# Slot attention inside one large kernel: the per-group tail work is put in other places on PE, ACT, DVE

## The reference, cut to what matters

```python
q  = slot_query                              # 16 slots, D = 256, the same for 32 batches
o  = q + mha(q, x, x, d_Wq, ..., d_Wo, d_bo)  # 16 heads; x: 32 batches of 64 tokens
h  = layernorm(o, e_ln_g, e_ln_b)             # per slot
u  = silu(h @ e_W1 + e_b1);  g = silu(h @ e_Wg + e_bg)     # 16 experts, one per slot
o  = o + (u * g) @ e_W2 + e_b2
out = mha(x, o, o, c_Wq, ..., c_Wo, c_bo)
```

## Time and profile before

| | us |
|---|---|
| median of 3 runs | 900.05 |
| lowest, highest | 898.2, 902.98 |
| the profiled execution | 898.2 |
| its span, first to last instruction | 896.2 |
| PE busy, of the span | 806.1 (90%) |
| DVE, ACT, POOL busy | 580.4, 511.6, 200.6 |
| first scores of `slots` / last work of `slots` / first expert matmul | 695.1 / 756.3 / 757.8 |

### The profile page before, as it was taken

The page is one execution under the profiler, slowest core; times in us unless marked ns, Lnnn a source line. Parts: engine busy times, 40 slices in busy tenths (PEclk is TensorE's granted clock), DMA queues, the critical chain, the costliest instruction groups (busy, mean ns, idle before and its releaser), DMA issues. The chain is left out here.

```text
span 896.2 us, 20582 instructions
## 1 busy us (share of the span) xinstructions
PE 806.1 (90%) x8104; PEld 696.4 (78%) x8104; DVE 580.4 (65%) x966; ACT 511.6 (57%) x954; POOL 200.6 (22%) x256
## 2 busy tenths in 40 slices
PE   5488999999999878999999998999997997997797
PEld 5278999999999756777778887999997995463454
DVE  3666777877877548888678884455443786331496
ACT  4138797888888526667577784433332454442354
POOL 0031433443433222244221223000000020000052
PEclk8689999999999989999999999999999999999899
DMA  7048676866876122442131103000000956999532
GB/s 301 6 167 307 249 257 225 308 229 219 288 271 212 49 76 55 87 89 47 37 135 33 49 25 103 39 2 1 1 1 12 409 242 222 423 426 420 204 93 72
DMA packets 70567, 143.20 MB, mean 160 GB/s; under 512 B 42521, under 2 KB 48153, under 8 KB 62921
## 3 DMA queue, kind: packets, MB, share of 16 engines
q1 hardware_dynamic: 64368, 127.25, 39.9%
q0 software_dynamic: 4496, 12.53, 4.0%
q10 hardware_dynamic: 1608, 2.12, 0.7%
HBM read 128.38 MB, written 13.50 MB: 158 GB/s over the span
## 5 line engine op out<-in xcount | busy, mean ns | idle before, releaser
L541 POOL DMA_INDIRECT results_of_experts<-k_w_ff,moew_place_of x39 | 53.5, 1371 | 148.8 <-DVE k_w_ff L769 86.9
L87 PE MATMUL moe_pH<-moe_hh,moew_wh 128*128 128x256 f32 x256 | 72.5, 283 | 2.4 <-DVE moe_hl L760 2.4
L89 PE MATMUL moe_pH<-moe_hl,moew_wh 128*128 128x256 f32 x256 | 71.7, 280 | 0.0
L88 PE MATMUL moe_pH<-moe_hh,moew_wl 128*128 128x256 f32 x256 | 71.7, 280 | 0.0
L760 DVE TENSOR_TENSOR moe_hl<-k_w_ff,moe_hh 128x512 fp32r<-128x512 f32 x64 | 44.3, 692 | 29.8 <-ACT moe_hh L697 29.8
L688 ACT ACTIVATE k_w_ff<-moe_pH,moew_b 128x256 f32<-128x256 f32 x128 | 53.3, 468 | 13.5 <-PE moe_pH L89 13.4
L740 DVE TENSOR_TENSOR moew_wl<-k_x,moew_wh 128x1024 fp32r<-128x1024 f32 x47 | 55.6, 1219 | 1.0 <-ACT moew_wh L660 1.0
L740 DVE TENSOR_TENSOR moew_wl<-moew_raw,moew_wh 128x1024 fp32r<-128x1024 f32 x44 | 52.2, 1219 | 5.8 <-ACT moew_wh L660 5.8
L1715 DVE TENSOR_TENSOR k_w_ff<-attn_pS,k_w_ff 128x512 f32<-128x512 f32 x32 | 22.1, 691 | 50.3 <-PE attn_pS L89 34.6
L87 PEld LDWEIGHTS moe_pH<-moe_hh,moew_wh 128*128 128x128 f32 x256 | 48.2, 188 | 4.0 <-DVE moe_hl L760 3.4
L87 PE MATMUL moe_pY<-moew_wh,moe_hh 128*128 128x256 f32 x156 | 46.5, 298 | 5.2 <-DVE moe_hl L755 2.6
(11 more groups left out here) (442 smaller groups left out, 2675.6 us busy)
## 6 DMA issues: line engine op xcount, KB each, us to landing
ring<-in_w_slot SPq DMA_DIRECT2D x10, 2048.0 KB, 15.9
k_x<-in_w SPq DMA_DIRECT2D x24, 512.0 KB, 5.2
k_x<-in_w SPq DMA_DIRECT2D x12, 1024.0 KB, 5.9
moew_raw<-in_w SPq DMA_DIRECT2D x22, 512.0 KB, 5.5
moew_raw<-in_w SPq DMA_DIRECT2D x11, 1024.0 KB, 6.1
ring<-in_w_slot SPq DMA_DIRECT2D x10, 1024.0 KB, 15.4
k_w_ff<-in_w_slot SPq DMA_DIRECT2D x4, 2048.0 KB, 10.6
attn_gat<-results_of_experts SPq DMA_DIRECT2D x16, 256.0 KB, 3.5
```

Of the source, the lines that this page charges most:

```text
L87: nc.tensor.matmul(out, ah, bh, start=start, stop=False)
L88: nc.tensor.matmul(out, al, bh, start=False, stop=False)
L89: return nc.tensor.matmul(out, ah, bl, start=False, stop=stop)
L541: nc.gpsimd.indirect_dma_start(out=dr.ys, out_offset=bass.IndirectOffsetOnAxis(ap=g.place_of[:, q:q + 1], axis=0), in_=ys[j % 2][:, s, :], ...
```

## The change

Four things are changed, all in `slots`. (1) `own_head` on DVE no longer adds the bias into `ob` in two operations; it writes the sum without bias, in one operation, to `g.oT` (semaphore `ot_ok`), and a new step `outputs(n)` on ACT adds the bias and fills `ob` for a whole group in two activations. (2) The steps of each group stand in other places: `turn_slots` and `turn_normal` of groups 0 and 1 at the end of bodies 4 and 6 on PE instead of inside 5 and 7; `project(2)` after `values(7)`; `end_turn(7)` behind `end(6)`; on ACT `squares` and `normal_turned` behind `exps` and `weights`, the activation that loads the Sqrt table inside body 7; on DVE `normalised` ahead of `own_head`, `based(0)` and `based(1)` behind `normal`, `summed(2)` and `scaled(2)` later. (3) At the end, `project(3)` stands ahead of `turn_normal(2)` with six idle transposes before it, and the last copy into `g.hT` is split between ACT and DVE. (4) PSUM places of the groups change accordingly, and `project(1)` and `project(2)` wait for `h_sb` and `b_sb`.

```diff
--- before.py
+++ after.py
@@ -1965,8 +1965,8 @@
         pT = ps("pT", [P, KD, 2, HS])
         pU = ps("pU", [P, 2, 512])
         m2_ok, x_ps, xh_ok, xl_ok, q_ps, q_sb, v_ps, v_sb = (sem(n) for n in ("m2_ok", "x_ps", "xh_ok", "xl_ok", "q_ps", "q_sb", "v_ps", "v_sb"))
-        s_ps, mx_ok, mc_ok, df_ok, ex_ok, sm_ok, rc_ok, pn_ok, pt_ps, pt_sb, u_ps, own_ok = (
-            sem(n) for n in ("s_ps", "mx_ok", "mc_ok", "df_ok", "ex_ok", "sm_ok", "rc_ok", "pn_ok", "pt_ps", "pt_sb", "u_ps", "own_ok"))
+        s_ps, mx_ok, mc_ok, df_ok, ex_ok, sm_ok, rc_ok, pn_ok, pt_ps, pt_sb, u_ps, own_ok, ot_ok = (
+            sem(n) for n in ("s_ps", "mx_ok", "mc_ok", "df_ok", "ex_ok", "sm_ok", "rc_ok", "pn_ok", "pt_ps", "pt_sb", "u_ps", "own_ok", "ot_ok"))
         q_out = [sem(f"q_out{a}") for a in range(2)]
         g.baseT = g.resT
         pN = ps("pN", [P, 2, D])
@@ -1982,13 +1982,13 @@
         rs = [sb(f"rs{n}", [P, 2]) for n in range(4)]
         base_ok, ob_ok, o_ps, o_ok, su_ok, nm_ok, og_ok, s2_ok, neg_ok, rs_ok, inv_ok = (
             sem(n) for n in ("base_ok", "ob_ok", "o_ps", "o_ok", "su_ok", "nm_ok", "og_ok", "s2_ok", "neg_ok", "rs_ok", "inv_ok"))
-        ms_ok, rv_ok, root_ok, xn_ok, r_ps, b_sb, h_ps, h_sb = (
-            sem(n) for n in ("ms_ok", "rv_ok", "root_ok", "xn_ok", "r_ps", "b_sb", "h_ps", "h_sb"))
+        ms_ok, rv_ok, root_ok, xn_ok, r_ps, b_sb, h_ps, h_sb, last_h_sb = (
+            sem(n) for n in ("ms_ok", "rv_ok", "root_ok", "xn_ok", "r_ps", "b_sb", "h_ps", "h_sb", "last_h_sb"))
         flat_s, flat_t = pS[:, :, :, :].rearrange("p c b k -> p (c b k)"), pT[:, :, :, :].rearrange("p c a n -> p (c a n)")
-        from_o = (pN[:, 0, :], pN[:, 0, :], pX[:, 0, :], pQ[:, 0, :])
-        from_slots = (pN[:, 1, :], pN[:, 1, :], pN[:, 1, :], flat_s[:, 0:D])
+        from_o = (pN[:, 0, :], pN[:, 0, :], pN[:, 0, :], pQ[:, 0, :])
+        from_slots = (pN[:, 1, :], pN[:, 1, :], pX[:, 0, :], flat_s[:, 0:D])
         from_normal = ([pN[:, 0, 0:P], pN[:, 0, P:2 * P]], [pN[:, 0, 0:P], pN[:, 0, P:2 * P]], [pVt[:, 0, 0:P], pVt[:, 0, P:2 * P]],
-                       [flat_t[:, 0:P], flat_t[:, P:2 * P]])
+                       [flat_t[:, 0:P], pN[:, 1, 0:P]])
 
         def by_slot(ap, n):
 
@@ -2114,8 +2114,8 @@
                     nc.tensor.transpose(flat_t[:, D:D + P], g.ident[:, :], g.ident[:, :])
 
             def project(n):
-                pe.wait_ge(ob_ok, KD * (2 * n + 2))
-                if n == 1:
+                pe.wait_ge(ob_ok, KD * (n + 1))
+                if 0 < n < 3:
                     pe.wait_ge(h_sb, KD * n)
                     pe.wait_ge(b_sb, KD * n)
                 if n == 3:
@@ -2126,9 +2126,6 @@
 
             def turn_slots(n):
                 pe.wait_ge(o_ok, n + 1)
-                if n == 2:
-                    pe.wait_ge(b_sb, KD * n)
-                    pe.wait_ge(h_sb, KD * n)
                 for c in range(KD):
                     last = nc.tensor.transpose(from_slots[n][:, c * P:(c + 1) * P], o[n % 2][:, c * P:(c + 1) * P], g.ident[:, :])
                 last.then_inc(r_ps, 1)
@@ -2144,25 +2141,23 @@
                 scores(i)
                 if i + 1 < NBODY:
                     turn(i + 1)
-                else:
-                    project(2)
-                if i in (5, 7):
-                    turn_slots((i - 5) // 2)
-                    turn_normal((i - 5) // 2)
                 queries(i)
                 if i > 0:
                     end_turn(i - 1)
                 values(i)
-                if i in (3, 5):
+                if i in (3, 5, 7):
                     project((i - 3) // 2)
-                if i == NBODY - 1:
-                    end_turn(i)
                 if i > 0:
                     end(i - 1)
+                if i in (4, 6):
+                    turn_slots((i - 4) // 2)
+                    turn_normal((i - 4) // 2)
+            end_turn(NBODY - 1)
             end(NBODY - 1)
             turn_slots(2)
+            idle(6)
+            project(3)
             turn_normal(2)
-            project(3)
             turn_slots(3)
             idle(10)
             turn_normal(3)
@@ -2200,6 +2195,14 @@
                     act.wait_ge(u_ps, i - 1)
                 nc.scalar.activation(vt[i % 2][:, :, :], pVt[:, :, :], ACT.Copy).then_inc(v_sb, 1)
 
+            def outputs(n):
+                act.wait_ge(ot_ok, 2 * n + 2)
+                if n > 0:
+                    act.wait_ge(o_ps, n)
+                for k in range(KD):
+                    nc.scalar.activation(ob[:, k, :], g.oT[:, k, 4 * n:4 * n + 4, :, :].rearrange("p a b s -> p (a b s)"), ACT.Identity,
+                                         bias=g.cols[:, COL_DBV, k:k + 1]).then_inc(ob_ok, 1)
+
             def squares(n):
                 act.wait_ge(nm_ok, n + 1)
                 if n > 0:
@@ -2212,27 +2215,30 @@
 
             def normal_turned(n):
                 act.wait_ge(h_ps, n + 1)
-                for c in range(KD):
+                for c in range(KD if n < 3 else 1):
                     nc.scalar.activation(by_slot(g.hT[:, c, :, :], n), by_batch(from_normal[n][c]), ACT.Copy).then_inc(h_sb, 1)
 
             high(0)
             for i in range(NBODY):
                 if i + 1 < NBODY:
                     high(i + 1)
+                exps(i)
+                if i > 0:
+                    weights(i - 1)
+                if i == NBODY - 1:
+                    nc.scalar.activation(warm[:, :], m2[:, 0:1], ACT.Sqrt)
                 if i in (4, 6):
                     squares((i - 4) // 2)
                 if i in (5, 7):
                     normal_turned((i - 5) // 2)
-                exps(i)
-                if i > 0:
-                    weights(i - 1)
-                if i == NBODY - 1:
-                    squares(2)
+                if i in (3, 5, 7):
+                    outputs((i - 3) // 2)
                 queries(i)
                 values(i)
-            nc.scalar.activation(warm[:, :], m2[:, 0:1], ACT.Sqrt)
             weights(NBODY - 1)
+            squares(2)
             root(2)
+            outputs(3)
             normal_turned(2)
             squares(3)
             root(3)
@@ -2272,16 +2278,13 @@
             def own_head(i):
                 dve.wait_ge(u_ps, i + 1)
                 if i > 0:
-                    dve.wait_ge(ob_ok, KD * i)
+                    dve.wait_ge(ot_ok, i)
                 v.tensor_tensor(own[:, :, :, :, :].rearrange("p x b u s -> p b x (u s)"), pU[:, :, 0:P].rearrange("p b (x n) -> p b x n", x=4),
                                 bc(bc(m32[:, :, :].rearrange("p u s -> p (u s)"), 1, 4), 1, 2), ALU.mult).then_inc(own_ok, 1)
                 dve.wait_ge(own_ok, i + 1)
-                if i in (2, 4, 6):
-                    dve.wait_ge(o_ps, i // 2)
-                for c in range(KD):
-                    v.scalar_tensor_tensor(ob[:, c, i % 2 * (P // 2):(i % 2 + 1) * (P // 2)].rearrange("p (x s) -> p x s", s=NS),
-                                           own[:, 2 * c:2 * c + 2, :, 0, :].rearrange("p a b s -> p (a b) s"), g.cols[:, COL_DBV, c:c + 1],
-                                           own[:, 2 * c:2 * c + 2, :, 1, :].rearrange("p a b s -> p (a b) s"), ALU.add, ALU.add).then_inc(ob_ok, 1)
+                v.tensor_tensor(g.oT[:, :, 2 * i:2 * i + 2, :, :].rearrange("p c a b s -> p c (a b) s"),
+                                own[:, :, :, 0, :].rearrange("p (c a) b s -> p c (a b) s", c=KD),
+                                own[:, :, :, 1, :].rearrange("p (c a) b s -> p c (a b) s", c=KD), ALU.add).then_inc(ot_ok, 1)
 
             v.tensor_reduce(m2[:, :], g.headmask[:, :].rearrange("p (q u) -> p u q", u=2), AX_X, ALU.add).then_inc(m2_ok, 1)
             dve.wait_ge(m2_ok, 1)
@@ -2329,34 +2332,33 @@
                 differences(i)
                 if i + 1 < NBODY:
                     low(i + 1)
-                else:
-                    summed(2)
-                if i == 5:
-                    based(0)
                 normal(i)
                 if i == 2:
                     dve.wait_ge(g.ffn_in, 16 * 5)
                     v.tensor_tensor(base, g.slot_tm[:, :], g.rows[:, ROW_DBO, :], ALU.add).then_inc(base_ok, 1)
                     dve.wait_ge(base_ok, 1)
-                if i == 7:
-                    based(1)
-                    scaled(2)
+                if i in (4, 6):
+                    normalised((i - 4) // 2)
+                if i in (5, 7):
+                    based((i - 5) // 2)
                 if i > 0:
                     own_head(i - 1)
+                if i in (3, 5, 7):
+                    summed((i - 3) // 2)
                 if i in (3, 5):
-                    summed((i - 3) // 2)
                     scaled((i - 3) // 2)
-                if i in (4, 6):
-                    normalised((i - 4) // 2)
             spread(2)
+            own_head(NBODY - 1)
+            scaled(2)
             normalised(2)
-            own_head(NBODY - 1)
             summed(3)
             scaled(3)
```

(2 more changed lines are left out.)

## The result

The changed kernel takes 913.33 us (median of 4 runs, 912.4 to 917.12) against 901.51 of the kernel before in the same runs: 1.0143 of it, 95% interval 1.01 to 1.0187. Ten further runs beside others of the kernel before gave 914.02 against 903.76, ratio 1.0105 [1.0074, 1.0137]. So it is slower, as forecast, but by 10 to 12 us where 7.5 were forecast, and 913.33 lies above the range of 903 to 911. The profiled execution has a span of 909.2 us (before 896.2), clock 0.961 (before 0.968).

The account below looks back on a forecast made before the run. PE was taken to bound the slots stage, passing delays one to one to the end; +5.6 us by the start of body 7 and +1.9 to project(3) made +7.5, so 900.05 became 907.5 us, range 903 to 911.

Parts of the forecast that it names:

- What bounds the kernel, and one to one to the end: Slots stage: PE is the bound, DVE and ACT close behind; any gain or loss there reaches the end one to one.
- Bodies 4 and 6, three moves on one chain: Late squares, earlier transposes, earlier normalised: PE waits for xn before turn_normal, a stall of 2.15 us in each body.
- 2.63 us from squares to `inv`: Bodies 4 and 6: time from start of squares through POOL's six operations to inv, taken as 2.63 us.
- Body 5: PE's project(1) waits for based(0), now behind normal(5): stall 1.06 us, body 7.98 us.
- Rival B: Stalls lower PE's clock: one or two falls of about 1.7 us, +9.2 to +11, 910; chance 0.08.
- Body 7 and tail: From scores(7) to project(3): project(2) stalls 2.2 us behind table load and based(1); 12.98 against 11.07, +1.9 us.
- The sum as a whole: Whole kernel: +5.6 us by the start of body 7 and +1.9 to project(3), +7.5 us; median forecast 907.5.
- Costs that no row shows: own_head's add 0.28 us, saving 0.1 per body; outputs 0.45; idle(6) free; extra DMA loads have slack; together +-0.6.
- The split of the last copy: Tail: last pair of copies split between ACT and DVE, nothing either way, +-0.2 us.
- Rival C: Outputs, queries: Identity not served by Sqrt's table, two or three reloads of 1.28 us: +4, to 911.5; chance 0.04.
- A: Bodies 4 and 6: inverse root ready when PE reaches turn_normal, so not slower: 899, no change; chance 0.14.
- D: Change does less: squares in time for one of two bodies, or project(1) not late: +4 to +5, 904.5; chance 0.06.

Follow-up runs that it names:

- shifted: Changed kernel with 8 dummy transposes ahead of turn_normal(0) in body 4: stretch (scores of body 3 to first streamed load) 57.10 us, ratio 1.0074 to the kernel before.
- load_late: Changed kernel with the Sqrt table load back behind values(7) on ACT: stretch 59.15 us, ratio 1.0176 to the kernel before.
- filled: Changed kernel with 18 dummy transposes before turn_normal of bodies 4 and 6, 14 before project(2): 908.42 us against 914.02, ratio 1.0048 to the kernel before.
- start_and_load: Kernel before with 2 dummy transposes ahead of turn(0), 12 behind it, Sqrt table load between exps(7) and weights(6): 899.26 us against 904.08, ratio 0.995.
- all_early: Changed kernel with squares, normal_turned and based early again and the Sqrt table load late: stretch 51.31 us, ratio 1.0027 to the kernel before.
- Turns_inside: Changed kernel with turn_slots and turn_normal of groups 0 and 1 back inside bodies 5 and 7 on PE: 906.9 us, stretch 54.61.

## Why the prediction was right in sign and wrong in size

- **What bounds the kernel, and one to one to the end**: right for the two kernels compared (136.4 and 136.5 us behind the first load before, 135.65 and 135.6 after). Twelve of the fourteen profiles have 135.1 to 137.5; shifted has 138.7 and load_late 140.0, both with a low clock behind the load (0.78 and 0.73 over its first 10 us, and again 0.64 and 0.59 over 10 us of `tokens`).
- **Bodies 4 and 6, three moves on one chain**: right in mechanism (2.29 and 2.32 against 2.15 us; down to 0.37 to 0.82 with either the squares or the transposes moved back). The term "2.63 us from squares to `inv`" was 3.09: POOL's first operation took 0.67 in all seven profiles with the late squares, where it runs beside DVE's product of two SBUF operands, and 0.19 in the seven others. The rows of before could not show it; the Trainium skill could (below).
- **Body 5**: the wait is there (1.00 us in filled, 1.06 forecast). The body was 0.98 longer than forecast, 0.84 of it because its scores and queries ran at a clock of 0.68 to 0.75. The failed step is that the sum put PE's clock behind the new gaps at nothing, on the ground "Against: from 748 to 758 PE is busy 4.65 of 10 us with clock 1.00": one profile of a tail that at other times falls. Rival B had the mechanism, with a chance of 0.08 and one or two falls of 1.7 us; by filled the clock cost 2.94 us in the stretch, 0.84 behind the first gap, 1.15 behind the second and 0.95 from project(3) on. It should have stood in the sum.
- **Body 7 and tail**, the term that was off most: +1.91 forecast, +4.00 measured, and +0.98 behind it. Of the 2.09 too much, 1.15 is the clock behind the second gap, 0.64 the gap inside end(7), and 0.30 sizes that were taken too small (outputs among them); the 0.98 behind is project(3) at half speed. Whether the gap in end(7), with which that goes in all ten profiles of this family, brings it is not shown. That end(7) now follows end(6) with 0.69 us of wait where it was 1.79 was taken for a gain (the table load off the way to weights(7)); what that wait had covered was not asked. In the kernel before, an instruction packet for PE lands at 748.59, inside the wait of 747.75 to 749.54.
- **The sum as a whole**: the stretch is 4.95 us above the forecast, and the clock's 2.94, the 0.64 of the gap in end(7) and the 1.4 left in filled make it up. But 46.08 was the better of two profiles of the kernel before, by 2.3 us; against the other the changed kernel is 10.1 longer, and to that extent the size of the miss is the luck of the draw.
- **Costs that no row shows**: own_head's add took 0.29, as forecast (0.28). Outputs took 0.69, between 0.45 and 0.83 but not the 0.45 that was taken; moved alone it added 0.9 us ahead of project(3) in one profile and nothing that the medians show. The table load costs 1.28 us, warm and next at +1.40, as the row said. The drain of about 1.38 us that the Trainium skill adds (ScalarE: Activation LUTs, section "What ACT_TABLE_LOAD costs") was not seen here either. The split of the last copy: nothing that shows (4.41 against 4.36).
- **Rival C** (Identity behind Sqrt's table): out, no second load. **A**, **D**: out.

What stays open: the medians favour filled by 2 us more than its stretch does, and start_and_load by 3 more than its parts; with one profile each I can't say where. Both profiles of the kernel before are of executions faster (898.2 and 899.97 us) than the medians of its runs (901.5 to 904.1), so what a typical run of it loses is not profiled. Why the gap inside end(7) is longer in one variant than in another is not shown.

## What to carry to other kernels

On an engine that is full, a step moved earlier must be followed back along everything it waits for; three moves that each look harmless made one chain of 4.7 us for which PE came 2.3 us too soon. Price each new gap on PE twice: for itself, and for slower matmuls behind it; and ask of each wait that goes what else it had covered. Dummies put in to test one thing move all later instructions: look what else went. One profile of a tail that idles is one draw: take two before a clock of 1.00 goes into a sum.

## What the runs showed of the hardware

- The gap of 2.3 us in body 4, on a PE otherwise full, was followed by a granted clock of 0.68 over 3 us in the changed kernel, 0.60 when it ran again, 0.50 with the load late (windows that begin at different distances from the gap); with 8 dummies in it (1.43 us left) or 18 it stayed at 1.00. Fifty dummies that do nothing gained 5.6 us in the medians and 3.55 in the stretch, 2.94 of that by the clock.
- PE can run out of instructions: it stood 0.50 to 1.94 us ahead of the last 6 of end(7)'s matmuls (six profiles of five kernels), and no longer when 8 transposes, 16 instructions, were put in long before. That it is the fetch of the next block is inferred, from three things. The gap moved with the place of the instruction. In all six profiles a 16 KB packet of kind instruction on DMA queue 8 (in the changed kernel from 759.93 to 760.83) lands 1.37 to 1.58 us before the gap ends, however long the gap. And all_early has a second, small gap of this kind, 0.19 us ahead of the last 13 of end(2)'s matmuls: counted in the trace, the second lies 1281 of PE's instructions behind the first, which is 5 times 256 and one. Turns_inside has as many instructions ahead of end(7) and no gap, and there the packet lands at 755.29, about 2.2 us before PE comes to the last 6. What passes in the 1.4 us behind the packet no trace shows. The Trainium skill, Runtime: NRT & Kernel Launch, section "Instruction fetch mechanics", says that instructions come in blocks of 256 and that the fetch is hidden since the engine issues more slowly than it is filled. The blocks of 256 agree with that count, and from the start of end(6) to the gap there are 252 instructions (64 and 58 matmuls and 4 transposes, each with its weight load). That the fetch is hidden does not hold here, where these 252 pass in 2.7 us.
- A POOL operation beside DVE's product of two SBUF operands took 0.67 us for 0.19 and ended 0.05 us after it, in each kernel with late squares. The Trainium skill, SBUF — State Buffer, section "Who interferes with whom", says that such a DVE instruction holds the read port that POOL needs; the trace agrees.
